# A mixture-of-experts feed-forward: low weight halves formed once per expert and copied into the slot ring by DMA

## The reference

```
shared   = silu(x @ shared_w1.T) @ shared_w2.T           # all 4096 tokens, hidden 512
gates    = softmax(top2(x @ gate_w.T))                   # two of 8 experts per token
expert e = silu(x @ experts_w1[e].T) @ experts_w2[e].T   # only its own tokens count
x_next   = x + layernorm(shared + sum_e gate_e * expert_e)
```

## Time and profile before

| | before |
|---|---|
| median of three runs | 1445.7 us |
| the profiled execution, device time | 1447.36 us |
| its span, first to last instruction | 1445.4 us |
| PE busy | 1299.3 us (90%) |
| DVE busy | 1124.2 us (78%) |
| ACT busy | 971.6 us (67%) |
| POOL busy | 759.6 us (53%) |
| stretch of the slots, first `slot_up` to last | 572.53 to 715.44 us |

### The profile page before, as it was taken

One profiled execution on the slowest core, in us unless ns is written; L12 is line 12 of the kernel. 1 busy time (PEld: TensorE's weight loads), 2 busy tenths in 40 slices (PEclk: granted clock), 3 DMA queues, 4 the chain that ended last, 5 costly groups with the idle time before them and its releaser, 6 DMA issues. The chain is left out here.

```text
span 1445.4 us, 34194 instructions
## 1 busy us (share of the span) xinstructions
PE 1299.3 (90%) x12121; PEld 988.3 (68%) x12121; DVE 1124.2 (78%) x3042; ACT 971.6 (67%) x1499; POOL 759.6 (53%) x973
## 2 busy tenths in 40 slices
PE   2799999999999779999928999999999998799996
PEld 1466666666655467889816777777777776688885
DVE  5578888888877657999857888888888776477776
ACT  1688888888887447777724777777777877444341
POOL 4775665788763364899775454455444330101112
PEclk9799999999999889999967999999999999899999
DMA  6000000011111120222122111111111110225253
GB/s 235 20 20 24 20 21 23 25 29 33 29 31 41 37 62 27 67 67 74 55 84 56 50 48 49 47 46 48 49 47 39 40 41 18 59 62 132 67 132 81
DMA packets 84429, 77.20 MB, mean 53 GB/s; under 512 B 18224, under 2 KB 72240, under 8 KB 83888
## 3 DMA queue, kind: packets, MB, share of 16 engines
q1 hardware_dynamic: 80176, 66.73, 17.4%
q0 software_dynamic: 4096, 8.40, 2.0%
HBM read 36.26 MB, written 13.63 MB: 35 GB/s over the span
## 5 line engine op out<-in xcount | busy, mean ns | idle before, releaser
L545 ACT ACTIVATE a_p<-a_ps_s 128x1024 f32<-128x1024 f32 x256 | 258.3, 1030 | 21.8 <-PE a_ps_s L404 21.5
L1318 DVE TENSOR_REDUCE a_qt<-a_ps_d 128x2 fp32r<-128x512 f32 x256 | 174.9, 690 | 42.8 <-PE a_ps_d L1097 37.1
L655 DVE TENSOR_REDUCE a_qt<-a_ps_d 128x2 fp32r<-128x512 f32 x256 | 174.6, 688 | 40.1 <-PE a_ps_d L415 38.4
L827 POOL TENSOR_TENSOR a_rn<-a_ss,a_half 128x16 f32<-128x16 f32 x56 | 162.9, 2926 | 1.3
L1219 ACT ACTIVATE a_pg<-a_ps_s 128x1024 f32<-128x1024 f32 x128 | 125.8, 1024 | 24.1 <-PE a_ps_s L1086 22.5
L422 PE MATMUL a_ps_o<-a_p,a_v 128*32 128x256 f32 x2048 | 127.4, 388 | 3.7 <-ACT a_p L545 3.7
L1097 PE MATMUL a_ps_d<-a_kpad,a_qs 128*128 128x512 f32 x256 | 126.3, 496 | 3.9 <-DVE a_qt L1318 1.5
L415 PE MATMUL a_ps_d<-a_kpad,a_qs 128*128 128x512 f32 x256 | 126.0, 493 | 2.7 <-DVE a_qt L655 2.3
L2412 ACT ACTIVATE f_s<-f_ps_g 128x512 f32<-128x512 f32 x72 | 43.1, 599 | 98.5 <-PE f_ps_g L2348 96.5
L1506 POOL DMA_INDIRECT a_picked<-ys,rows x64 | 67.5, 1055 | 61.5 <-PE a_ps_d L1097 50.6
L422 PEld LDWEIGHTS a_ps_o<-a_p,a_v 128*32 128x32 f32 x2048 | 60.4, 110 | 52.0 <-issue 20.5
(11 more groups left out here) (385 smaller groups left out, 3827.0 us busy)
## 6 DMA issues: line engine op xcount, KB each, us to landing
a_kpad<-a_kc SPq DMA_DIRECT2D x512, 32.0 KB
f_gb<-spread SPq DMA_DIRECT2D x64, 256.0 KB, 5.6
a_kpad<-a_kq SPq DMA_DIRECT2D x256, 32.0 KB, 1.8
f_xin<-xs SPq DMA_DIRECT2D x39, 128.0 KB, 2.1
ys<-f_yout SPq DMA_DIRECT2D x39, 128.0 KB, 2.1
w<-in_w SPq DMA_DIRECT2D x2, 2304.0 KB, 11.4
out_x<-X SPq DMA_DIRECT2D x8, 256.0 KB, 6.8
xs<-f_zero SPq DMA_DIRECT2D x15, 128.0 KB, 1.9
```

The costliest lines, as they stand in the source:

```text
L545: nc.scalar.activation(probs[:, u % 2, 2 * c:2 * c + 2, :, :].rearrange("p a b c -> p (a b c)"), ps_s[:, 2 * c:2 * c + 2, :].rearrange("p ...
L655: nc.vector.tensor_reduce(qt2[:, (k - PEAK) % 4, 2 * part:2 * part + 2, SHIFT], bank(k, f"m{part}")[:, :].rearrange("p (a b) -> p a b", b= ...
L827: nc.gpsimd.tensor_tensor(rn[:, part * c:(part + 1) * c], ss[:, part * c:(part + 1) * c], half[:, 0:c], ALU.pow).then_inc(rn_ready, 1)
L1318: nc.vector.tensor_reduce(qt[:, b % 2, GLOBAL, n:n + 2, SHIFT], bank(k, f"m{part}")[:, :].rearrange("p (j s) -> p j s", s=S), AX.X, ALU.ma ...
```

## The change

The low halves of w1 and of w2 of all eight experts are formed once, in the shared stage: POOL casts each matrix into `w2l` as a scratch place (`cast_into`), VectorE subtracts it from the matrix and writes `w1l` or, in place, `w2l` (`split_w1`, `split_w2`). In the slots POOL keeps only the two casts of the high halves. The low halves reach the ring by two DMAs from SBUF to SBUF per slot, 256 KB each, issued by SP (`low_w1`, `low_w2`); each reads the slot's expert from `table` into a register first. PE waits for the DMAs' semaphores. VectorE's subtraction per slot is gone.

```diff
                              ).then_inc(xin_loaded[n % AHEAD], 16)
 
+            def low_w1(n):
+                if n == 0:
+                    sp.wait_ge(w_lo, 2 + E)
+                else:
+                    sp.wait_ge(up_full, SHARED + 2 * max(n - 1, 0))
+                at = nc.sync.value_load(table[0:1, n:n + 1], min_val=0, max_val=(E - 1) * HID)
+                sp.dma_start(ring[:, n % 2, w1l_at].bitcast(F32), w1l[:, bass.ds(at, HID)].bitcast(F32)).then_inc(w1l_loaded[n % 2], 16)
+
+            def low_w2(n):
+                if n == 0:
+                    sp.wait_ge(w_lo, 2 + 2 * E)
+                else:
+                    sp.wait_ge(y_full, NT + n - 1)
+                at = nc.sync.value_load(table[0:1, n:n + 1], min_val=0, max_val=(E - 1) * HID)
+                sp.dma_start(ring[:, n % 2, w2l_at].bitcast(F32), w2l[:, bass.ds(at, HID)].bitcast(F32)).then_inc(w2l_loaded[n % 2], 16)
+
             for n in range(AHEAD):
                 load(n)
+            low_w1(0)
             for n in range(-1, SLOTS + BACK):
                 if AHEAD <= n + AHEAD + 1 < SLOTS:
                     load(n + AHEAD + 1)
@@ -1769,6 +1787,10 @@
                     sp.wait_ge(t_done, NT + m + 1)
                     sp.dma_start(a["ys"][m * SLOT_T:(m + 1) * SLOT_T, :].rearrange("(t p) d -> p t d", p=P),
                                  yout[:, m % 2, :, :]).then_inc(stored[m % 2], 16)
+                if n + 2 < SLOTS:
+                    low_w1(n + 2)
+                if n + 1 < SLOTS:
+                    low_w2(n + 1)
             for n in range(2):
                 sp.wait_ge(stored[n], 16 * ((SLOTS + 1 - n) // 2))
...
             def slot_up(n):
                 pe.wait_ge(xl_ready, NT + n + 1)
                 pe.wait_ge(w1_ready, n + 1)
+                pe.wait_ge(w1l_loaded[n % 2], 16 * (n // 2 + 1))
                 for h in range(2):
                     pe.wait_ge(silu_done, SHARED + max(2 * (n - 2) + h + 1, 0))
                     for c in (2 * h, 2 * h + 1):
@@ -1851,7 +1874,7 @@
 
             def slot_down(n):
                 pe.wait_ge(w2_ready, n + 1)
-                pe.wait_ge(w2l_ready, n + 1)
+                pe.wait_ge(w2l_loaded[n % 2], 16 * (n // 2 + 1))
                 wait(pe, y_done, NT + n)
...
             def split_w1(n):
-                dve.wait_ge(w1t_ready, n + 1)
-                nc.vector.tensor_tensor(w1l[:, n * HID:(n + 1) * HID], a["w1"][:, (n + 1) * HID:(n + 2) * HID],
-                                        w1t[:, n, :], ALU.subtract).then_inc(w_lo, 1)
+                cols, src = slice(n * HID, (n + 1) * HID), slice((n + 1) * HID, (n + 2) * HID)
+                dve.wait_ge(cast, n + 1)
+                nc.vector.tensor_tensor(w1l[:, cols], a["w1"][:, src], w2l[:, cols].bitcast(F32),
+                                        ALU.subtract).then_inc(w_lo, 1)
+
+            def split_w2(n):
+                cols, src = slice(n * HID, (n + 1) * HID), slice((n + 1) * HID, (n + 2) * HID)
+                dve.wait_ge(cast, E + n + 1)
+                nc.vector.tensor_tensor(w2l[:, cols], a["w2"][:, src], w2l[:, cols].bitcast(F32),
+                                        ALU.subtract).then_inc(w_lo, 1)
 
...
                     split_s(n, (1,))
-                    for e in {NT - 3: (n - 1, n), NT - 2: (n, n + 1), NT - 1: ()}.get(n, (n - 1,)):
+                    for e in {1: (0,), 2: (1, 2), 3: (3, 4), 4: (5, 6), 5: (7,)}.get(n, ()):
                         split_w1(e)
+                    for e in {5: (0, 1), 6: (2, 3, 4), 7: (5, 6, 7)}.get(n, ()):
+                        split_w2(e)
...
                 if 0 <= n < SLOTS:
-                    dve.wait_ge(w2_ready, n + 1)
-                    nc.vector.tensor_tensor(ring[:, n % 2, w2l_at], w2r[:, n % 2, :],
-                                            ring[:, n % 2, w2h_at].bitcast(F32), ALU.subtract).then_inc(w2l_ready, 1)
                     for h in range(2):
...
-            def split_w1(n):
-                nc.gpsimd.tensor_copy(w1t[:, n, :].bitcast(F32R), a["w1"][:, (n + 1) * HID:(n + 2) * HID]
-                                      ).then_inc(w1t_ready, 1)
-
-            for n in range(4):
-                split_w1(n)
+            def cast_into(n, w):
+                nc.gpsimd.tensor_copy(w2l[:, n * HID:(n + 1) * HID], w[:, (n + 1) * HID:(n + 2) * HID]
+                                      ).then_inc(cast, 1)
+
+            for n in range(E):
+                cast_into(n, a["w1"])
             pool.wait_ge(routed, AT)
             for i in range(GROUPS[-1][0] * TPB, TILES):
                 scatter(nc, Z, rt, i, a["xs"], scattered)
-            for n in range(4, E):
-                split_w1(n)
+            for n in range(E):
+                pool.wait_ge(w_lo, 2 + n + 1)
+                cast_into(n, a["w2"])
 
             def expert_of(n):
                 return nc.gpsimd.value_load(table[0:1, n:n + 1], min_val=0, max_val=(E - 1) * HID)
 
             def take_w1(n, at):
-                if n == 0:
-                    pool.wait_ge(w_lo, 2 + E)
-                elif n == 1:
+                if n == 1:
                     pool.wait_ge(up_full, SHARED)
-                else:
+                elif n > 1:
                     pool.wait_ge(up_full, SHARED + 2 * (n - 1))
-                nc.gpsimd.tensor_copy(ring[:, n % 2, w1h_at], a["w1"][:, HID:][:, bass.ds(at, HID)])
-                nc.gpsimd.tensor_copy(ring[:, n % 2, w1l_at], w1l[:, bass.ds(at, HID)]).then_inc(w1_ready, 1)
+                nc.gpsimd.tensor_copy(ring[:, n % 2, w1h_at], a["w1"][:, HID:][:, bass.ds(at, HID)]).then_inc(w1_ready, 1)
 
             def take_w2(n, at):
                 if n == 1:
                     pool.wait_ge(y_full, NT)
                 elif n > 1:
                     pool.wait_ge(y_full, NT + n - 1)
-                nc.gpsimd.tensor_copy(ring[:, n % 2, w2h_at], a["w2"][:, HID:][:, bass.ds(at, HID)])
-                nc.gpsimd.tensor_copy(w2r[:, n % 2, :], a["w2"][:, HID:][:, bass.ds(at, HID)]).then_inc(w2_ready, 1)
+                nc.gpsimd.tensor_copy(ring[:, n % 2, w2h_at], a["w2"][:, HID:][:, bass.ds(at, HID)]).then_inc(w2_ready, 1)
 
```

More of the change, by code:

```diff
@@ L1679, in first_ffn @@
         ring = sb("ring", [P, 2, 4 * HID], F32R)
-        w2r = sb("w2r", [P, 2, HID])
         s = sb("s", [P, 4 * TOK])
@@ L1694, in first_ffn @@
         pad_at = sb("pad_at", [P, EXPERTS], I32)
-        w1t = sb("w1t", [P, E, HID])
+        w2l = sb("w2l", [P, E * HID], F32R)
         y_late, yT = sb("y_late", [P, S]), sb("yT", [P, S])
@@ L1718, in first_ffn @@
         Z_MOVED, E2 = 1, 2
-        w_hi, w_lo, w1t_ready = sem("w_hi"), sem("w_lo"), sem("w1t_ready")
+        w_hi, w_lo, cast = sem("w_hi"), sem("w_lo"), sem("cast")
         up_full, silu_done, sh_done, sl_done = sem("up_full"), sem("silu_done"), sem("sh_done"), sem("sl_done")
@@ L1724, in first_ffn @@
         stored = [sem(f"stored{n}") for n in range(2)]
-        w1_ready, w2_ready, w2l_ready = sem("w1_ready"), sem("w2_ready"), sem("w2l_ready")
+        w1_ready, w2_ready = sem("w1_ready"), sem("w2_ready")
+        w1l_loaded = [sem(f"w1l_loaded{n}") for n in range(2)]
+        w2l_loaded = [sem(f"w2l_loaded{n}") for n in range(2)]
         block = ctx.enter_context(nc.Block(no_gpsimd_drain=True))
```

## The result

The changed kernel takes 1458.98 us, the median of six runs (1457.25 to 1464.21), against 1445.37 for the kernel before beside it. The ratio is 1.0094 with a 95% interval of 1.0078 to 1.0111: slower, by 13.6 us. The forecast was 1458 (1448 to 1470).

A forecast was written before the change was run, and what follows sets the result against it. Taken as the bound after the change: SP's issue list, about 4.15 us an iteration against PE's 3.38, putting slot 38 12.5 us later. 1445.7 + 12.5 = 1458.2, about 1458 us, range 1448 to 1470.

The forecast's parts named there:

- The bound: In the slots, SP's list of DMAs and register loads sets the pace at 3.9 to 4.5 us an iteration; chance 0.80.
- The rival by the sum of the records: SP's groups overlap or are shorter, 3.3 us an iteration or less; PE paces at 3.38, total 1434; chance 0.09.
- The cost of an iteration: SP per slot: token load 1.17, store 0.51, two low-half copies at 1.24 each, say 4.15 us.
- issue surcharge: Extra SP time to issue an SBUF to SBUF copy over the token load's 0.377: +0.07 us, bounds 0 and +0.21.
- between the register load's record and what uses the register: Where SP's missing 0.3 us per group, absent from the instruction records, was said to lie.
- The estimate by the floor of 600 ns: With about 600 ns per `tensor_load`, an SP group is 0.6 + 0.61 = 1.21 us and the iteration 4.28.
- Landing: A 256 KB low-half copy into the ring takes 2.9 us to land, ends 1.8 and 6.8.
- The onset: PE follows SP from slot 5 on, whose w1 copy lands at 592.5; PE without a wait would be there at 591.9.
- If every slot ran at 3.38: PE's 36 slot intervals at 3.38 instead of 3.73 us on average: 12.6 us shorter, the whole prize of the change.
- The slots in sum: Slot 38 starts at 727.9 against 715.44, later by 12.5 us, including 0.7 from the shared stage.
- The shared stage: DVE's added subtractions in block 7 delay the start of `slot_up(0)` by 0.7 us; POOL's casts beside the routing chain taken as 0.
- Blocks up to 6 have slack: Shared stage: DVE's one added 0.65 us subtraction in each of blocks 2 to 6 fits; 1.77 us of waiting left after block 6's pair.

The follow-up runs named there:

- e4: The changed kernel with one more register load from `table` per iteration on SP, its value unused: 1487.04 us, ratio 1.029.
- e3: The changed kernel with copies of 32 columns (16 KB) in place of 512 (256 KB), two memsets filling the rest of ring place 0: 1459.64 us, ratio 1.0098.
- e2: The changed kernel with both copies reading a fixed expert, no register load for them, so low halves are those of a wrong expert: 1441.16 us, ratio 0.997.
- e9: e7 with VectorE's copy of the previous result moved from behind both subtractions of a slot to between them: 1433.79 us, ratio 0.9899.
- e7: The changed kernel with both low halves copied into the ring by POOL, no transfer inside SBUF: 1439.68 us, ratio 0.9947.
- e8: The changed kernel with w1's cast in place in `w1l`, all sixteen POOL casts early and VectorE's subtractions redistributed over the blocks: 1460.61 us, ratio 1.0095.
- e1: The changed kernel with SP reading a slot's expert once and keeping the register for both copies: 1451.78 us, ratio 1.0045.

## Why the prediction came out

**The bound.** Right: SP's list sets the pace. e4 shows that it had no slack, e3 that bytes and landing do not matter, e2 that without the register loads the pace goes back to PE. The rival by the sum of the records (0.88 per group) is refuted: groups stand at 1.18 to 1.25.

**The cost of an iteration.** Predicted 1.17 + 0.51 + 2 x 1.24 = 4.15 (4.16 before rounding). Measured 4.05 undisturbed and 4.18 on the mean. Counted as the prediction did, from the end of one DMA to the end of the next, the token load is 1.15, the store 0.51 and the copies 1.21 and 1.18. The copy's issue surcharge was 0.12 instead of 0.07, but what stands between two DMAs is 0.69 to 0.76 where the prediction took 1.17 - 0.38 = 0.79 for each. The 0.13 between 4.05 and 4.18 are the irregular delays, which were no term of the sum. That the two errors cancel is luck.

The prediction also says where the time missing from the records lies, "between the register load's record and what uses the register". That reading was wrong: in the trace the first register instruction starts 0.03 us behind the load's record, and the missing 0.2 to 0.3 us are pauses of 0.03 to 0.06 between all the instructions of a group. The estimate by the floor of 600 ns for `tensor_load`, which the Trainium skill states (DMA: Bandwidth & Descriptors, "Latency and other measured facts"), came near in size, 1.21 for a group against 1.18 to 1.25. But no load of the changed kernel's steady slots is recorded near 0.6; those of L1758 take 0.264 to 0.274, so the measurement does not bear out the floor as the cause.

**Landing** 2.3, not 2.9: too high, without effect, as e3 shows.

**The onset.** Predicted at slot 5, at 592.5 after a slot 2 at 581.8, 10.7 us. Measured: 10.96 from slot 2 to slot 5, but PE first waits for a copy at slot 8. The step that failed is "If every slot ran at 3.38": between slots 2 and 7 the intervals are 3.81, 3.31, 3.84, 3.31 and 3.86. PE's own pace has a second wait in it, for VectorE's copy of the result, which the wait for `f_w2r` had covered. e2 (3.52 on the mean) and e9 (3.31 when it is moved) show it. The prize of the change was thus smaller than 12.6 us without e9's edit: 10.7 by e7. Nor was 3.38 a slot without a wait: e9 runs at 3.31.

**The slots in sum**: predicted 12.5 - 0.7 = 11.8 from `slot_up(0)` to `slot_up(38)`, measured 154.71 - 142.91 = 11.8. Slots 5 to 36 took 128.65 us, just the predicted 31 x 4.15, though PE did not wait for SP before slot 8 and the sum for the iteration holds two errors. So the agreement is luck in part. The total does show the error of the shared stage: forecast were 12.5 us, and it came to 14.8 from `up(0)` on in the profiled pair and to 13.6 in the medians.

**The shared stage.** Predicted 0.7, measured 2.7. "Blocks up to 6 have slack" failed: I counted VectorE's added 0.65 against its idle time and left out what POOL's casts do to the operations beside them (a subtraction at 2.09, two small ones at 0.57 and 0.53), though the earlier trace rows had the same effect. The routing chain was stretched by 1.1 us (one operation at 1.01, one at 0.53), above the 0 that I took, but PE's answer came earlier by 0.9, so nearly none of it passed on. The Trainium skill (SBUF — State Buffer, "SBUF: two separate sides") states that a VectorE operation with two SBUF inputs and a GpSimd operation that reads SBUF take a shared port pair as an exclusive lock for a whole instruction. The 7.09 us of e8 agree in kind and show more: VectorE's operation was passed by some twelve casts, so its wait is not bounded by one of them.

## What to carry to other kernels

Before work goes to an engine with idle time, add up that engine's list per iteration by intervals from start to start; busy time and record durations hide a part of each register load and issue. A sequencer that issues DMAs can be the bound like any other engine, and the view that shows it is its own timeline. And test the two halves of such a change apart: here forming the values once won 10.7 us in the slots, and carrying them by the wrong queue lost 22.7.

## What the runs showed of the hardware

- On SP the start of one DMA follows that of the DMA before it by 1.18 to 1.25 us with a register load from SBUF between them, and by 0.43 without; a further register load adds 0.76 us (e4), although its instructions are recorded with 0.43.
- A register load is recorded with 0.267 us behind one DMA, with 0.53 in the median behind two in a row (e1), and with 0.53 behind another register load (e4). Why is open.
- A transfer of 256 KB inside SBUF landed in 2.3 us, one of 16 KB in 1.7 (e3); its issue took SP 0.50 us.
- A VectorE operation of two SBUF operands can be kept out while many of POOL's casts pass: 7.09 us for one of 0.22, beside sixteen casts without a pause (e8).
